# Gate and up sums as seven block products instead of eight, over two blocks of 512 rows, with streamed weights

## The chip, the cores and the metric

The kernel runs on one core of one Trainium2 chip. The metric is the device time of one execution in microseconds (us), median of the runs. All matrix work goes through TensorE; VectorE (DVE in the profile), ScalarE (ACT) and GpSimd (POOL) do the elementwise work, SyncE (SP) issues the DMAs. Each engine has one queue of instructions and works through it in order; a wait on a semaphore holds all that stands behind it in that queue.

## The reference

An array x of 2048 rows by 512 columns passes through five stages, each a residual update of x with a LayerNorm in front:

```
x = x + 0.5 * L0_ffn(layernorm(x))    # a 6-bit quantised 512x512 linear layer with bias
x = x + L0_attn(layernorm(x))         # causal convolution along the 512 columns, as a Toeplitz product
x = x + 0.5 * L0_ffn(layernorm(x))
x = x + 0.5 * L1_ffn(layernorm(x))    # the gated layer below
x = x + L1_attn(layernorm(x))         # convolution again, another filter
x = x + 0.5 * L1_ffn(layernorm(x))

def _L1_ffn_ref(x, W_gate, W_up, W_down):      # W_gate, W_up: 1376 x 512, W_down: 512 x 1376
    up = xt @ W_up.T
    gate = jax.nn.silu(xt @ W_gate.T)
    y = gate * up @ W_down.T
```

So there are six stages. The gated layer is run twice with the same weights; its hidden width 1376 is 10 blocks of 128 and one of 96. All arithmetic is float32.

## The kernel before

**Precision.** TensorE works in fp32r, a rounded float32. Each operand is therefore held as two parts, hi (the rounded value) and lo (the value minus hi), and each product is three matmuls: hi by hi, hi by lo, lo by hi. ScalarE makes hi by a copy, VectorE or GpSimd makes lo by a subtraction.

**Tiles and stages.** x stays in SBUF as 16 tiles of 128 rows (`x_rows`). Stages 0 to 2 (quantised, convolution, quantised) and 4 (convolution) are light: per tile 12 matmuls (`products`, L909 to L911), and 4 transposes of the normalised tile four items ahead (`transpose_step`, L312). Stages 3 and 5 are the gated layer.

**The way of a tile.** VectorE takes the statistics (`stats_step`, L271; `aggregate_step`, L281), GpSimd makes 1/sqrt(variance) and the shift by four tiny operations (`rstd_step`, L288 to L295), ScalarE normalises (`norm_step`, L305), TensorE transposes into a PSUM bank (L312), ScalarE rounds to `xt_hi` (L322), VectorE subtracts to `xt_lo` (L327), and after the products VectorE adds the sum to x (`update_step`, L335, L337). In the quantised stages GpSimd also adds a bias to each x tile (`bias_step`, L442) ahead of the update. Statistics run 7, GpSimd 6, the normalisation 5 (NORM_AHEAD) and the transposes 4 items ahead.

**Weights.** The gate, up and down weights are loaded once, in 32 chunks of 520 columns (`load_chunk`, L372), split while stages 1 and 2 run (ScalarE `chunk_hi_step` L534; lo on GpSimd L448 for the first 16 chunks, on VectorE L838 for the rest), and stay in SBUF, hi and lo, for both gated stages.

**Gated stages.** Four blocks of 512 rows each (BLK = 4 tiles), 11 steps f per block. In a step TensorE makes the gate and the up sum of hidden block f (`paired_sums`: stage 3 L997 to L1004, stage 5 L1008 to L1015; the first step of a stage `hidden_sums`, L980 to L982): 4 blocks of 128 input columns x 3 x 2 = 24 matmuls of 512 columns. Then it makes the down sums of step f-1 (`down`, L1038 to L1040): 4 row tiles x 3 = 12 matmuls, into the four `acc` banks, which add up over all 11 steps. Gate and up sums use four `front` banks, two a step in turn. Beside it ScalarE applies silu to the gate (L620), VectorE multiplies by up (L864), ScalarE rounds (L630), VectorE subtracts (L869). At a block's end 16 transposes prepare the next rows, then comes the last down.

**Code.** Stage 0 is straight code; stages 1 to 5 are loops over groups of four tiles or blocks (Fori), with the first block of each gated stage and the last of stage 5 apart.

## Time and profile before

| | |
|---|---|
| Time, median of 3 runs | 968.42 us (968.04 to 968.46) |
| Profiled execution | 968.6 us, span of its instructions 966.8 us |
| Busy: PE, DVE, ACT, POOL | 941.0, 361.5, 258.5, 189.6 us |
| Matmuls | 4376 |
| Mean granted TensorE clock | 0.996 |
| DMA moved | 21.70 MB, mean 22 GB/s |

How to read it: a share is busy time over the span. The duration that the profile gives for a matmul includes its way through the array, about 0.39 us for 512 columns, and the next one starts long before that; the cost of a matmul in a stream is the distance from its start to the next start. A granted clock of 1.0 means 2.4 GHz. Lines (L997) are lines of the kernel printed above.

### The profile page before, as it was taken

To read this page: it belongs to the slowest core of one execution; us is meant where nothing else is said; L and a number is where in the kernel's file an instruction comes from. 1 tells how busy PE (TensorE), PEld (TensorE's weight loads), DVE (VectorE), ACT (ScalarE), POOL (GpSimd) and SP (SyncE) were. 2 spreads that over 40 slices of the span, in tenths; PEclk is the share of its full clock that TensorE was granted. 3 is DMA by queue.
4 is the path that set the end of the run, shared out by engine and by line. 5 is a ranking of instruction groups with operands and counts; after the bars stand their busy time and mean duration, and the time that the engine had idled before them with its cause. 6 is when DMAs were issued, how large, how long until landed. Compare 5 with 4: busy or idle time off the path is not lost.

```text
span 966.8 us, 12613 instructions
## 1 busy us (share of the span) xinstructions
PE 941.0 (97%) x4376; PEld 771.8 (80%) x4376; DVE 361.5 (37%) x671; ACT 258.5 (27%) x415; POOL 189.6 (20%) x491
## 2 busy tenths in 40 slices
PE   3898999999999999999999999999999999999998
PEld 2675988888888878887888899888888788888886
DVE  6787869722132213221322286221321132223112
ACT  3432765422121212211221244121211122122111
POOL 5974899601000000100010033000000001000000
PEclk9999999999999999999999999999999999999999
DMA  8100333100000000000000000000100010001001
GB/s 311 67 1 0 89 96 89 58 1 1 0 1 1 1 1 0 0 0 0 0 0 0 0 0 1 1 1 1 44 0 1 1 43 0 0 0 44 1 1 43
DMA packets 10799, 21.70 MB, mean 22 GB/s; under 512 B 1040, under 2 KB 1296, under 8 KB 10768
## 3 DMA queue, kind: packets, MB, share of 16 engines
q1 hardware_dynamic: 10768, 21.28, 6.7%
q8 instruction: 20, 0.33, 0.1%
q14 instruction: 11, 0.09, 0.0%
HBM read 17.08 MB, written 4.19 MB: 22 GB/s over the span
## 4 chain that ended last, share of the span: by engine, by line
PE 86%; POOL 2%; DVE 1%; issue 1%; DMA 1%; ACT 1%; POOLq 0%; ACTq 0%; SPq 0%; DVEq 0%
PE acc L1038 8%; PE acc L1040 8%; PE acc L1039 8%; PE front L997 4%; PE front L1008 4%; PE front L1004 4%; PE front L1015 4%; PE front L998 4%; PE front L1009 4%; PE front L1000 4%; PE front L1013 4%; PE front L1010 4%; PE front L999 4%; PE front L1014 4%; PE front L1001 4%; PE front L312 3%
## 5 line engine op out<-in xcount | busy, mean ns | idle before, releaser
L864 DVE TENSOR_TENSOR gated<-front,gated 128x512 f32<-128x512 f32 (+1 forms) x88 | 60.8, 691 | 492.3 <-ACT gated L620 262.1
L620 ACT ACTIVATE gated<-front 128x512 f32<-128x512 f32 (+1 forms) x88 | 52.7, 599 | 493.5 <-PE front L1010 246.7
L288 POOL TENSOR_TENSOR minus_mean<-mean_var,constant_columns 128x1 f32<-128x1 f32 x98 | 25.3, 258 | 606.1 <-DVE mean_var L281 606.1
L1038 PE MATMUL acc<-ffn_w_hi,hidden_hi 128*128 128x512 f32 (+1 forms) x352 | 137.9, 392 | 0.0
L1040 PE MATMUL acc<-ffn_w_hi,hidden_lo 128*128 128x512 f32 (+1 forms) x352 | 137.0, 389 | 0.0
L1039 PE MATMUL acc<-ffn_w_lo,hidden_hi 128*128 128x512 f32 (+1 forms) x352 | 137.0, 389 | 0.0
L869 DVE TENSOR_TENSOR hidden_lo<-gated,hidden_hi 128x512 fp32r<-128x512 f32 (+1 forms) x88 | 60.9, 692 | 52.5 <-ACT hidden_hi L630 52.5
L305 ACT ACTIVATE normalised<-x_rows,minus_mean_rstd,rstd 128x512 f32 (+1 forms) x97 | 78.3, 808 | 4.4 <-POOL minus_mean_rstd L295 4.1
L322 ACT ACTIVATE xt_hi<-front 128x512 fp32r<-128x512 f32 x96 | 54.7, 595 | 89.5 <-PE front L312 89.4
L1040 PEld LDWEIGHTS acc<-ffn_w_hi,hidden_lo 128*128 128x128 f32 (+1 forms) x352 | 66.1, 188 | 14.1
L1039 PEld LDWEIGHTS acc<-ffn_w_lo,hidden_hi 128*128 128x128 f32 (+1 forms) x352 | 66.1, 188 | 14.0
L630 ACT ACTIVATE hidden_hi<-gated 128x512 fp32r<-128x512 f32 (+1 forms) x88 | 55.7, 633 | 80.7 <-DVE gated L864 80.7
L1038 PEld LDWEIGHTS acc<-ffn_w_hi,hidden_hi 128*128 128x128 f32 (+1 forms) x352 | 66.1, 188 | 13.9
L312 PE MATMUL front<-identity,normalised 128*128 128x128 f32 x384 | 57.1, 282 | 16.9 <-ACT normalised L305 16.8
L327 DVE TENSOR_TENSOR xt_lo<-front,xt_hi 128x512 fp32r<-128x512 f32 x96 | 63.9, 684 | 15.5 <-ACT xt_hi L322 14.4
L997 PE MATMUL front<-xt_hi,ffn_w_hi 128*128 128x512 f32 (+1 forms) x172 | 68.3, 397 | 0.0
L1008 PE MATMUL front<-xt_hi,ffn_w_hi 128*128 128x512 f32 (+1 forms) x172 | 68.3, 397 | 0.0
L1004 PE MATMUL front<-xt_hi,ffn_w_lo 128*128 128x512 f32 (+1 forms) x172 | 68.0, 396 | 0.0
L1015 PE MATMUL front<-xt_hi,ffn_w_lo 128*128 128x512 f32 (+1 forms) x172 | 68.0, 396 | 0.0
L998 PE MATMUL front<-xt_hi,ffn_w_hi 128*128 128x512 f32 (+1 forms) x172 | 67.4, 392 | 0.0
L1009 PE MATMUL front<-xt_lo,ffn_w_hi 128*128 128x512 f32 (+1 forms) x172 | 67.4, 392 | 0.0
L271 DVE BATCH_NORM_STATS2 bn_stats<-x_rows 128x6 f32 (+1 forms) x99 | 66.6, 673 | 1.8 <-DMA x_rows<-x_in 1.7
(148 smaller groups left out, 1654.9 us busy)
## 6 DMA issues: line engine op xcount, KB each, us to landing
gated<-wffn SPq DMA_DIRECT2D x32, 260.0 KB, 2.6
x_rows<-x_in SPq DMA_DIRECT2D x3, 1024.0 KB, 12.8
out<-x_rows SPq DMA_DIRECT2D x3, 1024.0 KB, 4.3
x_rows<-x_in SPq DMA_DIRECT2D x2, 512.0 KB, 6.3
q_raw<-qweight SPq DMA_DIRECT2D x4, 256.0 KB, 8.4
out<-x_rows SPq DMA_DIRECT2D x4, 256.0 KB, 2.1
omega_terms<-omega_in SPq DMA_DIRECT2D x1, 768.0 KB, 10.1
small_tables<-table_in SPq DMA_DIRECT2D x1, 517.0 KB, 10.7
```

What stands on the lines that cost most here:

```text
L271: nc.vector.bn_stats(bnst[:, slot, :], x_tile(t, ahead)).then_inc(stats_raw, 1)
L305: nc.scalar.activation(LN[:, slot, :], x_tile(t, ahead), ACT.Identity, bias=nmr[:, slot, :], scale=rstd[:, slot, :]).then_inc(norm_done, 1)
L312: last = nc.tensor.transpose(front[slot][:, j * P:(j + 1) * P], LN[:, slot, j * P:(j + 1) * P], ident[:])
L997: T.matmul(pair[0], hi[0], xh, start=first, stop=False)
L998: T.matmul(pair[1], hi[1], xh, start=first, stop=False)
L1004: up = T.matmul(pair[1], lo[1], xh, start=False, stop=final)
L1008: T.matmul(pair[0], hi[0], xh, start=first, stop=False)
L1009: T.matmul(pair[0], hi[0], xl, start=False, stop=False)
L1015: up = T.matmul(pair[1], lo[1], xh, start=False, stop=final)
L1038: T.matmul(acc[r][:], hh, Wh[:m, cols], start=(f == 0), stop=False)
L1039: T.matmul(acc[r][:], hh, Wl[:m, cols], start=False, stop=False)
L1040: last = T.matmul(acc[r][:], hl, Wh[:m, cols], start=False, stop=(f == FT - 1))
```

## The change

**Two blocks at a time.** A unit is now 8 tiles of 1024 rows: the tiles with an even place in the unit are one block of 512 rows (first half), the odd ones another (second half). There are 4 units: rows 0 to 1023 and 1024 to 2047, for each of the two gated stages. The gate and up sums of both row blocks are a 2 x 2 block product (gate and up by the two halves of the 512 input columns, by the two row blocks). Winograd's form of it takes 7 block products instead of 8, with 4 sums of weight blocks (S1 to S4) and 4 sums of row blocks (T1 to T3, T4N). Each product is 2 x 3 = 6 matmuls of 512 columns, so a step f has 42 matmuls where two blocks had 48. The products alternate between two PSUM banks (front 0 and 1). VectorE puts the four results together with seven adds, each of which reads a bank once.

**Weights are streamed.** SBUF no longer holds all of them. Each step loads 512 KB of gate and up weights (two slots) and each down pass 256 KB (three slots), in every unit again. Per step GpSimd makes four sums of 256 columns (`weight_sums`) and two subtractions of 1024 and 512 columns, ScalarE three roundings of 768, 1024 and 512, VectorE one subtraction of 768. The chunk splitting of stages 1 and 2 is gone.

**Down.** The first half's hidden blocks are rounded and summed as before, one step behind. The second half's hidden blocks (g1 x u1, made on GpSimd) are kept in float32 for all 11 steps (`second_hidden`, 22 KB a partition) and are rounded and summed in 11 passes after the steps, in the same four acc banks.

**Rows.** 8 tiles of a unit are prepared in 4 pairs (`pair_copies`, `pair_sums`, `pair_lows`, `sums_hi_step`, `sums_lo_step`): for unit 0 among the last items of stage 2, for the others between the down passes of the unit before. The layer-1 convolution (stage 4) is embedded in units 1 and 2: one item's products per step in steps 2 to 9, its transposes in steps 1 to 8. LayerNorm of coming items stands in the steps as the table `LN_OF_STEP` says. All code is straight, with no loops.

```diff
+UNITS = 4
+UTILES = 8
+STEPS = UNITS * FT
+PASSES = 2 * FT
+WD_RING = 3
...
+    after = {8: (0, 1), 10: (2, 3), 11: (4, 5), 12: (6, 7)}
+    for t in range(TILES):
+        light("quant", 0, t)
+        for p in after.get(t, ()):
+            prep(p)
...
+EMBEDDED = {0: 0, 1: UTILES, 2: UTILES, 3: 0}
+LN_OF_STEP = {u: {f: [] for f in range(FT)} for u in range(UNITS)}
+for _u in range(UNITS - 1):
+    for _e in range(EMBEDDED[_u]):
+        LN_OF_STEP[_u][_e].append(UNIT_ITEMS[_u] + _e)
+    for _s in range(BLK):
+        _f = 7 + _s if EMBEDDED[_u] else 3 + _s
+        for _i in range(2):
+            LN_OF_STEP[_u][_f].append(UNIT_ITEMS[_u] + EMBEDDED[_u] + 2 * _s + _i)
+PAIR_BEFORE_PASS = {-1: 0, 1: 1, 3: 2, 5: 3}
...
         @block.gpsimd
+            for n in range(PRE):
+                if ITEMS[n].kind == "quant":
+                    bias_step(n)
+                if n + RSTD_AHEAD < PRE:
+                    rstd_step(pool, n + RSTD_AHEAD)
...
+                if n + 3 < PRE and second_of_pair(n + 3):
+                    sums_lo_step(pool, ITEMS[n + 3].number // 2)
+                if n == PRE - 7:
+                    weight_sums(pool, 0)
+                if n == PRE - 4:
+                    weight_sum_lo(pool, 0)
+                    down_weight_lo(pool, 0)
...
+            def second_hidden(k):
+                f, u = k % FT, k // FT
+                pool.wait_ge(silu_done, 2 * k + 2)
+                pool.wait_ge(front_read, READS * k + C22)
+                if u:
+                    pool.wait_ge(hid_ready, PASSES * (u - 1) + FT + f + 1)
+                TT(H1[:, f, :], g1, u1, ALU.mult).then_inc(h1_made, 1)
+            for u in range(UNITS):
+                for f in range(FT):
+                    k, q = FT * u + f, PASSES * u + f
+                    if f:
+                        second_hidden(k - 1)
+                    if k + 1 < STEPS:
+                        weight_sums(pool, k + 1)
+                    down_weight_lo(pool, q + 1)
+                    if k + 1 < STEPS:
+                        weight_sum_lo(pool, k + 1)
+                    for n in LN_OF_STEP[u][f]:
+                        rstd_step(pool, n)
...
         @block.scalar
+            for u in range(UNITS):
+                for f in range(FT):
+                    k, q = FT * u + f, PASSES * u + f
+                    if f:
+                        silu(k - 1, g1, C12)
+                    snapshot(k)
+                    silu(k, g0, C11)
+                    if k + 1 < STEPS:
+                        weight_raw_hi(act, k + 1)
+                        weight_sum_hi(act, k + 1)
+                    down_weight_hi(act, q + 1)
+                    if 1 <= f <= EMBEDDED[u]:
+                        xt_hi_step(act, embedded_item(u, f - 1))
+                    for n in LN_OF_STEP[u][f]:
+                        norm_step(act, n)
+                    act.wait_ge(first_made, k + 1)
+                    hidden_hi(q, g0)
+                silu(FT * u + FT - 1, g1, C12)
+                if u + 1 < UNITS:
+                    pair_copies(act, BLK * (u + 1))
+                second_hidden_hi(u, 0)
+                for j in range(FT):
+                    q = PASSES * u + FT + j
+                    if u + 1 < UNITS and j in (0, 2, 4, 6):
+                        sums_hi_step(act, BLK * (u + 1) + j // 2)
+                    if q + 1 < UNITS * PASSES:
+                        down_weight_hi(act, q + 1)
+                    if u + 1 < UNITS and j in (1, 3, 5):
+                        pair_copies(act, BLK * (u + 1) + (j + 1) // 2)
+                    if j + 1 < FT:
+                        second_hidden_hi(u, j + 1)
...
         @block.vector
+                    first_gate(k)
+                    middle_sums(k)
+                    if k + 1 < STEPS:
+                        weight_raw_lo(dve, k + 1)
+                    if f == 0 and u:
+                        for r in range(BLK):
+                            ffn_update(u - 1, 1, r)
...
+                    first_hidden(k)
+                    second_gate(k)
+                    hidden_lo(q, g0)
+                q1 = PASSES * u + FT
+                hidden_lo(q1, H1[:, 0, :])
+                if u + 1 < UNITS:
+                    pair_sums(dve, BLK * (u + 1))
+                for r in range(BLK):
+                    ffn_update(u, 0, r)
+                if u + 1 < UNITS:
+                    pair_lows(dve, BLK * (u + 1))
+                for j in range(1, FT):
+                    hidden_lo(q1 + j, H1[:, j, :])
+                    if u + 1 < UNITS and j in (2, 4, 6):
+                        pair_sums(dve, BLK * (u + 1) + j // 2)
+                        pair_lows(dve, BLK * (u + 1) + j // 2)
...
         @block.tensor
+            for u in range(UNITS):
+                for f in range(FT):
...
+                    pe.wait_ge(w_raw_ready, k + 1)
...
+                    product(k, M1, A11, B11)
...
+                    product(k, M2, A12, B21)
...
+                    pe.wait_ge(w_sum_ready, k + 1)
+                    pe.wait_ge(snap_done, k + 1)
+                    product(k, M6, S2, T2)
+                    pe.wait_ge(front_read, READS * k + C11)
+                    product(k, M5, S1, T1)
+                    pe.wait_ge(front_read, READS * k + U2)
+                    product(k, M7, S3, T3)
+                    if 2 <= f < 2 + EMBEDDED[u]:
+                        embedded_products(embedded_item(u, f - 2))
...
+                    elif f:
+                        down(q - 1, ALL)
+                    if 1 <= f <= EMBEDDED[u]:
+                        embedded_transposes(embedded_item(u, f - 1))
+                    pe.wait_ge(front_read, READS * k + T_SUM)
+                    product(k, M4, A22, T4N)
+                    pe.wait_ge(front_read, READS * k + C22)
+                    product(k, M3, S4, B22)
...
+                for j in range(-1, FT - 1):
+                    if u + 1 < UNITS and j in PAIR_BEFORE_PASS:
+                        pair_transposes(BLK * (u + 1) + PAIR_BEFORE_PASS[j])
+                    down(PASSES * u + FT + j, ALL)
```

In the names: M1 to M7 are the products; C11, C12 the gate sums g0 and g1 of the two halves, C21, C22 the up sums; U2, U3 and T_SUM sums between. `snapshot` is ScalarE's copy of M1 out of its bank; M6 writes that bank next. The first half's hidden block g0 x up is made on VectorE (`first_hidden`), rounded by `hidden_hi` and subtracted by `hidden_lo`.

## Rows read from the trace of the kernel before

**Rows 1.** busy us, share of the span, and instructions by engine, from the page

```profile
PE 941.0 (97%) x4376; PEld 771.8 (80%) x4376; DVE 361.5 (37%) x671; ACT 258.5 (27%) x415; POOL 189.6 (20%) x491
```

**Rows 2.** table by stage: us, each engine's busy (instructions), PEclk, DMA share, GB/s

```profile
25.00:50.00 25.00, 23.11 (x105) 18.28 (x106) 18.94 (x35) 11.50 (x19) 23.01 (x63) 0.93 0.14 52
200.00:225.00 25.00, 25.00 (x111) 20.50 (x110) 6.25 (x13) 5.11 (x8) 2.14 (x8) 1.00 0.00 1
```

**Rows 3.** TensorE's longest wait: total us, times, longest

```profile
PE front L312 <- ACT normalised L305: 16.8, 6, 10.9
```

**Rows 4.** timeline of TensorE, stage 3: start us, duration, engine, line, operation

```profile
300.77 0.39 PE L997 MATMUL front<-xt_hi,ffn_w_hi 128*128 128x512 f32 x1
...
306.30 0.39 PE L1038 MATMUL acc<-ffn_w_hi,hidden_hi 128*128 128x512 f32 x1
...
309.03 0.39 PE L997 MATMUL front<-xt_hi,ffn_w_hi 128*128 128x512 f32 x1
```

**Rows 5.** chain that ended last, light stages: start us, us, what

```profile
108.39 0.55 POOL rstd L292
...
110.98 0.55 POOL rstd L292
...
140.06 0.44 PE front L312 x4
143.27 0.44 PE front L312 x4
...
560.91 0.46 PE front L312 x4
563.25 0.46 PE front L312 x4
```

**Rows 6.** groups by line and shape, VectorE and ScalarE: busy, mean ns, idle before

```profile
L869 DVE TENSOR_TENSOR hidden_lo<-gated,hidden_hi 128x512 fp32r<-128x512 f32 x80 | 55.4, 692 | 46.3 <-ACT hidden_hi L630 46.3
...
L793 DVE TENSOR_TENSOR toeplitz_f<-toeplitz_f,small_tables 128x128 f32<-128x128 f32 x2 | 0.6, 291 | 0.1
...
L305 ACT ACTIVATE normalised<-x_rows,minus_mean_rstd,rstd 128x512 f32 x72 | 58.2, 809 | 0.3
...
L630 ACT ACTIVATE hidden_hi<-gated 128x512 fp32r<-128x512 f32 x80 | 50.6, 633 | 73.5 <-DVE gated L864 73.5
...
L558 ACT ACTIVATE silu_of_a_constant<-constant_columns 128x1 f32<-128x1 f32 x1 | 0.2, 202 | 0.0
```

**Rows 7.** the same view for GpSimd, 128 columns

```profile
L483 POOL TENSOR_TENSOR inv_den_r<-den_r,den_tmp 128x128 f32<-128x128 f32 x4 | 1.8, 458 | 0.0
```

**Rows 8.** timeline of VectorE and GpSimd, stage 2, where two operations meet

```profile
141.18 1.29 POOL L442 TENSOR_TENSOR x_rows<-x_rows,half_bias 128x512 f32 x1
...
141.60 1.43 DVE L838 TENSOR_TENSOR ffn_w_lo<-gated,ffn_w_hi 128x520 f32 x1
...
142.43 0.65 POOL L288 TENSOR_TENSOR minus_mean<-mean_var,constant_columns 128x1 f32<-128x1 f32 x1
```

**Rows 9.** timeline of GpSimd, stage 2: one rstd_step and one bias_step

```profile
178.56 0.19 POOL L288 TENSOR_TENSOR minus_mean<-mean_var,constant_columns 128x1 f32<-128x1 f32 x1
...
179.80 1.29 POOL L442 TENSOR_TENSOR x_rows<-x_rows,half_bias 128x512 f32 x1
181.06 0.18 POOL L288 TENSOR_TENSOR minus_mean<-mean_var,constant_columns 128x1 f32<-128x1 f32 x1
```

**Rows 10.** DMA issues: queue, count, KB each, median us from issue to landing

```profile
gated<-wffn SPq DMA_DIRECT2D x32, 260.0 KB, 2.6
...
out<-x_rows SPq DMA_DIRECT2D x3, 1024.0 KB, 4.3
```

**Rows 11.** timeline of TensorE, stage 0, after a gap

```profile
27.10 0.66 PE L312 MATMUL front<-identity,normalised 128*128 128x128 f32 x4 [1.14 <-ACT normalised L305]
...
27.83 0.63 PE L910 MATMUL acc<-dequant_lo,xt_hi 128*128 128x512 f32 x1
...
30.81 0.59 PE L911 MATMUL acc<-dequant_hi,xt_lo 128*128 128x512 f32 x1
```

1095 lines of the change are left out of this document (606 added, 489 removed).

## The prediction

> **What bounds the kernel now.** I read the page's busy shares first: TensorE is busy 941.0 of 966.8 us, every other engine under 40% [rows 1]. That number can hide gaps, since matmul ends are modelled, so I read the table by stage next [rows 2]: in a feed-forward stretch (200 to 225 us) TensorE is busy all 25 us, VectorE 6.25, ScalarE 5.11, GpSimd 2.14. The list of TensorE's waits confirms it: 16.8 us in all behind the first normalised tiles and nothing in the feed-forward blocks [rows 3]. So the pitch of the matmuls is the price of the work. In the timeline [rows 4] 24 gate and up matmuls take 306.30 - 300.77 = 5.53 us, 0.2304 each, and 12 down matmuls 309.03 - 306.30 = 2.73 us, 0.2275 each. Eight blocks of 11 x 36 such matmuls are the 740 us that matter. The reader should see two things: removed matmuls are worth their full pitch, and the other engines have much free time but have so far handed over only once per 8.3 us.
>
> **What is removed.** Before: 8 blocks x 11 x 24 = 2112 gate and up matmuls. After: 4 units x 11 steps x 7 products x 6 = 1848. 264 fewer, x 0.2304 = 60.8 us. The pitch of the new products is not in the trace; its nearest rows are the old gate and up matmuls (0.2304, the same as now: no further gain) and the down matmuls (0.2275: 1848 x 0.0029 = 5.4 us more). I take the middle, 2.7. The downs, the 96 items' transposes and the light matmuls keep their number. The layer-1 convolution moves into steps 1 to 9 of units 1 and 2 at its own TensorE price: 2.34 us an item [rows 5], bound by TensorE then and later, so zero; nothing has to hide it.
>
> The weight split leaves the light stages. In the first convolution GpSimd's chunk set the pace, 110.98 - 108.39 = 2.59 us an item, where the second needs 563.25 - 560.91 = 2.34 [rows 5]: 16 x 0.25 = 4, of which I take 3 (0 to 4). Gains together: 60.8 + 2.7 + 3 = 66.5 us (61 to 70).
>
> **What is added, per step.** One step is 42 x 0.2304 + 12 x 0.2275 = 12.4 us of TensorE (14.7 with an embedded item). Sizes come from two rows each [rows 6], [rows 7]: VectorE 0.29 at 128 columns and 0.69 at 512, so 0.43 at 256 and 0.96 at 768; ScalarE 0.20 at one and 0.63 at 512, so 0.42 at 256 and 1.06 at 1024; GpSimd 0.46 at 128 and 1.29 at 512, so 0.74 at 256 and 2.40 at 1024. Per step VectorE has nine operations of 0.69 and one of 0.96, 7.2 us; ScalarE 4 x 0.63, 0.63, 0.85 and 1.06, 5.1; GpSimd 1.29 + 4 x 0.74 + 1.29 + 2.40 = 7.9. All fit under 12.4. The products themselves alternate between two banks: a product lasts 1.38 us and its last add 0.69 + 0.2, so each bank is free in time; M7's two adds and M5's are covered by the down sums that stand behind M7. So a bare step costs nothing by throughput; what costs is the order on each queue.
>
> The long loop runs ScalarE, GpSimd, ScalarE: second_hidden 1.29, weight_sums 3.1 with its waits, then weight_sum_hi and down_weight_hi 1.9 (GpSimd's down_weight_lo waits for both), 1.29, weight_sum_lo 2.40; VectorE's first_hidden 0.7 and add C12 0.7; silu of g1 0.7, which second_hidden of the next step waits for. That is 12.1 us, against 12.4.
>
> **The shared resource.** The timeline shows a VectorE subtraction of two SBUF operands take 1.43 us instead of 0.69: it begins 0.42 us into a GpSimd operation and ends 0.56 after it; GpSimd's next tiny operation in turn takes 0.65 instead of 0.19, up to VectorE's end [rows 8]. Per step three VectorE operations are of that kind (weight_raw_lo, first_hidden, hidden_lo). weight_raw_lo falls beside down_weight_lo and pushes weight_sum_lo by about 0.8: the loop becomes 12.9, 0.5 over TensorE. In 15 plain steps 0 to 8 us; I take 4.5, since the loop must first use up some slack. The Trainium skill, "SBUF — State Buffer", section "Who interferes with whom", calls this an exclusive lock held for the whole instruction. By it the wait behind a 1024-column weight_sum_lo or sums_lo could be the whole of it, which no row shows; that is the lock rival below.
>
> **LayerNorm in the steps.** rstd_step stands last on GpSimd's step, norm_step on ScalarE stands ahead of hidden_hi, and hidden_hi ahead of silu(g1) and of the next snapshot, for which M6 waits. A rstd_step is 179.80 - 178.56 = 1.24 us [rows 9], a norm 0.81 [rows 6]. With two items the loop is 12.9 + 2.5 + 0.8 + 0.6 - 1.4 (the adds no longer on it) = 15.4, less about 0.3 because operations queued back to back overlap: 15.1. Unit 0 has four such steps over 12.4: 4 x 2.7 - 2 of first slack = 8.5 us (5 to 11). Units 1 and 2: step 0, where four updates wait for the down sums and sit ahead of C21, 2; step 1, 1; step 7 with three items against 14.7, 1.5; steps 8 and 9, 0.5: 5 each, 10 together (6 to 16).
>
> **The second half of a unit.** 11 down passes of 2.73 us. Ahead of the first, on ScalarE, stand pair_copies (four operations, 1.5 to 1.8 us), which wait for the transposes, then the hidden's rounding; on VectorE hidden_lo, then pair_sums (1.7), then the updates that free the acc banks. Counted from the transposes' end: 1.5 + 0.7 + 0.7 + 1.7 + 0.7 = 5.3 us to the first freed bank, under 2.6 us of down sums: 2.7 late. For each later pair the loop copies 1.5, rounding 0.7, hidden_lo 0.6, pair_sums 1.7, sums_hi 1.0, and three half-us roundings is 7.0 us, against 2 x 2.73 + 0.9 = 6.4, and hidden_lo of the odd pass waits for sums_lo (2.40) to end, 1 to 2 us. Together 8.6 us for the change from unit 0. In units 1 and 2, step 10 still has two norms ahead of hidden_hi, so the last first-half hidden and the copies come some 4 us later: 12 each. Sum 33 (18 to 42). Unit 3 has no pairs: 0. A down weight's load (256 KB, 2.6 us to landing [rows 10]), ScalarE 0.6 and GpSimd 1.3 make 4.6 us after the pass that frees its slot, against two passes, 5.5: hidden, though only just. The 512 KB load of a step is put between 2.6 and 4.3 (260 and 1024 KB, [rows 10]), and has most of a step; it stands behind a down load whose wait ends earlier.
>
> **The end of the light part.** Eight preparation items stand among the last 15. An item of the quantised stage leaves GpSimd 0.7 us (2.50 of 3.21, [rows 9], [rows 5]). From item 38 on GpSimd has 12 x 1.24 + 7 x 1.29 + 4 x 2.40 (sums_lo) + 3.1 (first weight_sums) = 36.6 us before bias_step of item 50 has gone through, and xt_lo of items 54 and 55 stands behind that item's update on VectorE; TensorE wants them after 28 us and cannot run far ahead, because each preparation item waits for its pair. I take 12 us (4 to 14). The opening steps add 1.5.
>
> **The clock.** After a gap of 1.14 us TensorE ran eight matmuls 0.43 us apart [rows 11], the lower of its two levels (1.2 against 2.4 GHz); the granted clock of that stretch is 0.93 [rows 2]. Where it idles behind a loop of other engines the slower matmuls are absorbed; I add 3.5 us (0 to 25).
>
> **Sum.** 968.6 (the profiled execution; span 966.8, 0.2 over the median 968.42) - 66.5 + 4.5 + 8.5 + 10 + 33 + 12 + 1.5 + 3.5 = 975.1. Forecast: 975, slightly slower.
>
> **Rivals.** (1) The hand-offs hide. Should ScalarE and GpSimd pipeline better than my single file, the costs take their lower ends: 0 + 5 + 6 + 18 + 4 + 1 + 0 = 34, so 936, or 932 with the better pitch. For it: the free shares of [rows 2]; I followed queues in strict order with full latencies. Against: each chain is written out in the queues. (2) The lock decides, the slower side. From the point where second_hidden ends later than 5 us into a step, first_hidden meets weight_sum_lo from its beginning: 2.4 us before C12 instead of 0.5, in all 40 steps some 1 us more, 40 us: 1015. Against: VectorE may come first and push GpSimd instead, which costs 0.7. (3) The clock: 25 gaps over 1 us, each with 8 slower matmuls x 0.2 = 1.6, cost 40 rather than 3.5, half of it absorbed: 995. (4) The change does not do what it says, as weights come late: 44 loads, 1 us late each, 44 us less slack: 1000. Against: landing near 3.4 us in a 12.4 us step.
>
> **Chances.** Forecast 0.45, rival 1 0.33, rival 2 0.09, rival 3 0.09, rival 4 0.04. About 0.2% (2 us) is what a measurement of this kernel tells from no change. All of rival 1 and 0.05 of the forecast's share are faster, 0.05 lies within: faster 0.38, same 0.05, slower 0.57. The forecast's own range is 958 to 992. With both signs held, the range is 937 to 1005: it leaves out rival 1's lower edge and rival 2's.
>
> **What would show it.** Right: idle time of TensorE at M6 behind the snapshot in steps with LayerNorm, at the first second-half pass behind the updates, at the last light items behind xt_lo; steps near 12.9 and 15 us, the change of units 9 to 12 us over 27 + 2.7. Wrong: those waits absent and steps at 12.4 (rival 1); first_hidden with a mean over 1.5 us (rival 2); granted clock under 0.95 through the units (rival 3); waits on DMA at the weight roundings (rival 4). The saving itself is wrong if the products' pitch is off 0.23.

## The result, and the profile after

The changed kernel takes 996.6 us (median of 4 runs, 995.2 to 997.8) against 968.4: a ratio of 1.029 (1.027 to 1.031). The forecast was 975 us, slightly slower. The sign holds, and so does the range of 937 to 1005 us that takes in the rivals. The forecast's own range, 958 to 992, is missed, and so is the size: +28 us where +6.5 was forecast. I compare the two profiled executions, 996.6 and 968.6 us, whose spans differ by the same 28.0 us. One execution of one kernel below fell into a slower state of the chip (1361.6 us at a granted clock of 0.61) and is left out.

The head of the page, which answers [rows 1]:

```profile
span 994.8 us, 11946 instructions
PE 903.6 (91%) x4088; PEld 731.2 (74%) x4088; DVE 642.2 (65%) x1021; ACT 410.9 (41%) x650; POOL 634.4 (64%) x835
```

TensorE has less to do and is no longer always busy; VectorE and GpSimd went from 37% and 20% of the span to 65% and 64%. No engine but TensorE is near full, and the 91% still hides gaps. The same table by stage as [rows 2], with one more stretch:

```profile
25.00:50.00 25.00, 23.51 (x109) 19.15 (x110) 18.36 (x34) 12.46 (x20) 23.46 (x62) 0.93 0.21 83
200.00:225.00 25.00, 23.14 (x96) 18.35 (x95) 13.87 (x18) 8.11 (x12) 15.33 (x16) 0.95 0.07 22
175.00:200.00 25.00, 15.76 (x68) 12.55 (x69) 13.09 (x29) 12.34 (x19) 20.14 (x35) 0.85 0.00 0
```

From 175 to 200 us TensorE has work for 15.76 of 25 us, and its granted clock is 0.85: that is the end of the light part. Its waits, which answer [rows 3] (total, times, longest):

```profile
PE front L440 <- ACT normalised L433: 19.0, 9, 4.4
PE acc L1245 <- DVE hidden_lo L1118: 16.2, 13, 4.1
PE front L1291 <- DVE snapshots L1084: 12.1, 9, 3.1
PE front L1291 <- ACT snapshots L839: 10.1, 8, 2.3
PE front L440 <- DMA identity<-table_in: 9.3, 1, 9.3
PE acc L1245 <- POOL down_lo L569: 9.1, 9, 1.1
```

Before, nothing in the feed-forward blocks appeared in this view. Now the down passes wait for `hidden_lo` and `down_lo`, the products for the snapshot and the gate and up sums, the transposes for the norm. None waits on a weight load directly, though ScalarE's rounding of down weights does, 40.9 us in 23 times, 20 of them in the down passes behind the steps, and `down_lo` comes behind it.

The pitch, the counterpart of [rows 4]: four products of six matmuls in step 3 of unit 1 (start, duration; two such rows per product).

```profile
442.66 0.39 PE L1291 MATMUL front<-row_operands_hi,weight_operands_hi 128*128 128x512 f32 x1
...
444.02 0.39 PE L1291 MATMUL front<-row_operands_hi,weight_operands_hi 128*128 128x512 f32 x1
...
448.10 0.39 PE L1291 MATMUL front<-row_operands_hi,weight_operands_hi 128*128 128x512 f32 x1
```

Six matmuls take 1.36 us, 0.2267 each, a little better than the middle I took (about 0.229). A bare step therefore costs 54 x 0.2267 = 12.24 us, one with an embedded item 14.63.

What the steps really take is read from the first product's row in steps 4, 5, 6 and 7 of unit 0:

```profile
254.50 0.47 PE L1291 MATMUL front<-row_operands_hi,weight_operands_hi 128*128 128x512 f32 x1 [0.17 <-DVE snapshots L1084]
271.90 0.47 PE L1291 MATMUL front<-row_operands_hi,weight_operands_hi 128*128 128x512 f32 x1 [0.70 <-DVE snapshots L1084]
285.54 0.47 PE L1291 MATMUL front<-row_operands_hi,weight_operands_hi 128*128 128x512 f32 x1
302.95 0.47 PE L1291 MATMUL front<-row_operands_hi,weight_operands_hi 128*128 128x512 f32 x1 [0.71 <-DVE snapshots L1084]
```

17.4, 13.6, 17.4 us instead of 12.24. With every step read like this, the 28.0 us lie as follows. The first feed-forward product starts at 205.07 instead of 185.33: 19.7 us later. From there to the last matmul it is 786.2 us instead of 777.9: 8.3 us more, made of some 69 us saved (60.8 by matmuls not run, 8 by pitch) and some 80 us of steps and passes over their TensorE time, which agrees to 3 us. TensorE's time is counted at 0.2267 us a matmul, 2.39 an embedded item and 0.1 a transpose:

| Stretch | over TensorE's time | forecast |
|---|---|---|
| End of the light part | 24 (5 ahead when the second quantised stage began, 19.7 late at the end) | 12 (4 to 14) |
| Unit 0, steps 3 to 7 (LayerNorm in them) | 13.7 | 8.5 (5 to 11) |
| Units 1 and 2, steps 0 to 9 | 15 | 10 (6 to 16) |
| Three unit changes, with the step ahead of each | 40 | 33 (18 to 42) |
| Plain steps and the rest, unit 3 and the first step among them | 11 | 6: 4.5 (0 to 8) and 1.5 for the opening steps |

### The profile page after: what moved, and what is told of

Read it like the earlier page. It is cut to its first block, busy times and chain, and to the rows that moved or that the text cites. A ratio compares the mean times of both kernels' runs of the same rounds, so it can differ in the third digit from the quotient of the medians.

```text
span 994.8 us, 11946 instructions
## 1 busy us (share of the span) xinstructions
PE 903.6 (91%) x4088; PEld 731.2 (74%) x4088; DVE 642.2 (65%) x1021; ACT 410.9 (41%) x650; POOL 634.4 (64%) x835
## 4 chain that ended last, share of the span: by engine, by line
PE 55%; POOL 19%; DVE 12%; ACT 6%; issue 6%; DMA 3%; SPq 0%; POOLq 0%; DVEq 0%; ACTq 0%
PE front L1291 10%; PE front L1293 10%; PE front L1292 10%; PE acc L1245 5%; PE acc L1247 5%; PE acc L1246 4%; POOL down_lo L569 3%; POOL row_operands_lo L516 3%; POOL w_and_weight_operands_lo L559 3%; PE front L440 2%; PE acc L1185 2%; POOL rstd L422 2%; PE acc L1184 2%; PE acc L1183 2%; DVE w_and_weight_operands_lo L554 2%
## 5 line engine op out<-in xcount | busy, mean ns | idle before, releaser
L1291 PE MATMUL front<-row_operands_hi,weight_operands_hi 128*128 128x512 f32 x616 | 247.4, 402 | 23.1 <-DVE snapshots L1084 12.1
L1293 PE MATMUL front<-row_operands_hi,w_and_weight_operands_lo 128*128 128x512 f32 x616 | 243.5, 395 | 0.0
L1292 PE MATMUL front<-row_operands_lo,weight_operands_hi 128*128 128x512 f32 x616 | 243.3, 395 | 0.0
L569 POOL TENSOR_TENSOR down_lo<-raw_down,down_hi 128x512 fp32r<-128x512 f32 x88 | 131.8, 1499 | 141.6 <-ACT down_hi L564 133.0
L1245 PE MATMUL acc<-down_hi,hidden_hi 128*128 128x512 f32 x352 | 143.0, 406 | 27.1 <-DVE hidden_lo L1118 16.2
L1291 PEld LDWEIGHTS front<-row_operands_hi,weight_operands_hi 128*128 128x128 f32 x616 | 117.6, 191 | 58.6 <-issue 28.0
L1247 PE MATMUL acc<-down_hi,hidden_lo 128*128 128x512 f32 x352 | 138.8, 394 | 0.0
L1246 PE MATMUL acc<-down_lo,hidden_hi 128*128 128x512 f32 x352 | 138.8, 394 | 0.0
L1292 PEld LDWEIGHTS front<-row_operands_lo,weight_operands_hi 128*128 128x128 f32 x616 | 117.6, 191 | 23.3
L559 POOL TENSOR_TENSOR w_and_weight_operands_lo<-raw_weights,weight_operands_hi 128x1024 fp32r<-128x1024 f32 x44 | 117.6, 2672 | 0.0
L1247 PEld LDWEIGHTS acc<-down_hi,hidden_lo 128*128 128x128 f32 x352 | 66.9, 190 | 14.6
L440 PEld LDWEIGHTS front<-identity,normalised 128*128 128x128 f32 x384 | 47.0, 146 | 38.2 <-issue 14.6
## 6 DMA issues: line engine op xcount, KB each, us to landing
x_rows<-x_in SPq DMA_DIRECT2D x3, 1024.0 KB, 13.6
```

The costliest lines, as they stand in the source:

```text
L440: last = nc.tensor.transpose(o[:, j * P:(j + 1) * P], LN[:, n % LN_SLOTS, j * P:(j + 1) * P], ident[:])
L559: nc.gpsimd.tensor_tensor(flat(Wl, k, 1 + S1, 2 + S4), flat(Wr, k, 1 + S1, 2 + S4), flat(Wh, k, S1, S4 + 1).bitcast(F32), ALU.subtract).th ...
L569: nc.gpsimd.tensor_tensor(WDl[:, q % WD_RING, :], WDr[:, q % WD_RING, :], WDh[:, q % WD_RING, :].bitcast(F32), ALU.subtract).then_inc(wd_r ...
L1245: T.matmul(acc[r][:], hh, wh, start=(f == 0), stop=False)
L1246: T.matmul(acc[r][:], hh, wl, start=False, stop=False)
L1247: last = T.matmul(acc[r][:], hl, wh, start=False, stop=(f == FT - 1))
```

## The experiments

Each kernel below is the changed one with the edit shown; times are medians of 4 runs (3 in one case), beside 996.6 for the changed kernel. The kernel before, run again beside each of them, took 967.9 to 968.2. They are told nearly in the order in which they were run. "The steps" are the distances between first products, as above; step 10, the last, ends where the first down pass behind it starts, and "the passes" run from there to the next unit.

**Order in the light part.** VectorE, ScalarE and GpSimd:

```
-    pair_sums(dve, ...); pair_lows(dve, ...)
     aggregate_step(dve, n + STATS_AHEAD)
+    pair_sums(dve, ...); pair_lows(dve, ...)
...
+    sums_hi_step(act, ...)
     norm_step(act, n + NORM_AHEAD)
-    sums_hi_step(act, ...)
...
-    if n + 3 < PRE and second_of_pair(n + 3):
+    if n + 2 < PRE and second_of_pair(n + 2):
         sums_lo_step(pool, ...)
```

> Light part only: VectorE's aggregate stands ahead of the pair's sums instead of behind them, ScalarE's rounding of the pair sums ahead of the next norm, and GpSimd's sums_lo one item later, behind the next bias addition. No operation is added or removed. If the stall at the end of the light part (about 23 us in the changed kernel) comes from a ring of in-order queues (aggregate behind pair sums, rstd behind the aggregate, norm behind rstd, bias behind sums_lo), the first feed-forward product comes 8 to 15 us earlier than 205 us and the time is 982 to 989 us. If GpSimd's sheer work there is the bound, nothing moves: 995 to 998 us.

Measured 982.5 (980.3 to 986.1), 14.1 less; the first product starts at 194.22 instead of 205.07. The ring can be read in the changed kernel on one pair. GpSimd, after its bias addition, idles for VectorE's `aggregate`; then, much later, the 2.35 us `sums_lo` stands ahead of the next bias addition:

```profile
164.58 1.28 POOL L689 TENSOR_TENSOR x_rows<-x_rows,half_bias 128x512 f32<-128x512 f32 x1
168.26 0.19 POOL L418 TENSOR_TENSOR minus_mean<-mean_var,constant_columns 128x1 f32<-128x1 f32 x1 [2.40 <-DVE mean_var L413]
...
171.79 2.35 POOL L516 TENSOR_TENSOR row_operands_lo<-pair_sums,row_operands_hi 128x1024 fp32r<-128x1024 f32 x1 [2.30 <-ACT row_operands_hi L512]
174.10 1.26 POOL L689 TENSOR_TENSOR x_rows<-x_rows,half_bias 128x512 f32<-128x512 f32 x1
```

VectorE's aggregate stood behind the six operations of a pair (from 165.62 on) and began at 168.01; its next update but one waited 3.94 us for the bias addition. The waits between 145 and 205 us, of the changed kernel and of this one:

```profile
POOL minus_mean L418 <- DVE mean_var L413: 10.6, 6, 4.1
DVE x_rows L462 <- POOL x_rows L689: 20.6, 6, 7.4
PE front L440 <- ACT normalised L433: 13.3, 5, 4.4
```

```profile
POOL minus_mean L418 <- DVE mean_var L413: 4.1, 3, 3.0
DVE x_rows L462 <- POOL x_rows L689: 7.0, 4, 3.5
PE front L440 <- ACT normalised L433: 7.7, 4, 2.3
```

With not one operation fewer, 11 of the 24 us go. The stretch that my term added up can be read too: from GpSimd's bias addition of item 38 to that of item 50, in the changed kernel and in this one.

```profile
147.88 1.29 POOL L689 TENSOR_TENSOR x_rows<-x_rows,half_bias 128x512 f32<-128x512 f32 x1
...
195.19 1.28 POOL L689 TENSOR_TENSOR x_rows<-x_rows,half_bias 128x512 f32<-128x512 f32 x1
```

```profile
148.32 1.29 POOL L689 TENSOR_TENSOR x_rows<-x_rows,half_bias 128x512 f32<-128x512 f32 x1
...
183.38 1.27 POOL L689 TENSOR_TENSOR x_rows<-x_rows,half_bias 128x512 f32<-128x512 f32 x1
```

To the end of the second row that is 48.6 us in the changed kernel, of which GpSimd idles 15, and 36.3 us here, close to the 36.6 of my sum. So GpSimd's work was not what made the stretch long, since GpSimd itself stood idle. What remains (13 us) is close to the 12 I took, but I did not take it apart; nor the 3 us that the units gain in this kernel, where nothing was moved.

**The norm behind the rounding.**

```
-    for n in LN_OF_STEP[u][f]: norm_step(act, n)
     act.wait_ge(first_made, k + 1)
     hidden_hi(q, g0)
+    for n in LN_OF_STEP[u][f]: norm_step(act, n)
```

> In every step the LayerNorm of the items prepared there is put on ScalarE behind the rounding of the first hidden rows instead of ahead of it. Theory: in steps 3 to 6 of unit 0 and step 10 of units 1 and 2 the norms, which wait for GpSimd's rstd, delay hidden_hi, silu of g1 and the next snapshot; they cost 13.7 + 2 x 5.2 us there. Then this gives 12 to 20 us back: 976 to 985 us. Rival: those steps are long because GpSimd's own queue is (rstd behind a weight_sum_lo of 2.67 us, lengthened by VectorE's shared access): 0 to 4 us, 992 to 997 us.

Measured 1001.0 (1000.0 to 1001.8), 4.4 more. My theory fell: steps 3 to 7 of unit 0 are unchanged to 0.06 us. Silu of g1 and the snapshot stand behind the norm wherever in the step it is put, and the norm waits for its rstd. In units 1 and 2, step 10 fell to 15.4 but the passes after it grew from 41.7 to 45.5 us and more: the wait only moved.

**The updates first, at the unit change.**

```
-    pair_copies(act, BLK * (u + 1))
     second_hidden_hi(u, 0)
+    pair_copies(act, BLK * (u + 1))
...
-    pair_sums(dve, BLK * (u + 1))
     for r in range(BLK): ffn_update(u, 0, r)
+    pair_sums(dve, BLK * (u + 1))
```

> At each unit change the first second-half hidden rows are rounded ahead of the pair's four copies on ScalarE, and the four row updates stand ahead of the pair's sums on VectorE. Theory: the order of the two queues makes the first passes late, 2 to 4 us at each of three changes: 984 to 991 us. Rival: the passes are late because VectorE's hidden_lo waits for GpSimd's long sums_lo and ScalarE's copies for each other, whatever the order: within 2 us of the changed kernel, 994 to 998 us. A loss is possible if the pair's sums, now later, hold the next transposes.

Measured 1001.9 (998.2 to 1003.7), 5.3 more: the loss that I had called possible, but the rows suggest another reason (only a part of it, as the smaller edits on top of the three moves show). ScalarE in this kernel:

```profile
356.96 0.39 ACT L482 ACTIVATE row_operands_hi<-front 128x256 fp32r<-128x256 f32 x1
361.32 1.06 ACT L512 ACTIVATE row_operands_hi<-pair_sums 128x1024 fp32r<-128x1024 f32 x1 [3.97 <-DVE pair_sums L500]
362.29 0.61 ACT L564 ACTIVATE down_hi<-raw_down 128x512 fp32r<-128x512 f32 x1
362.80 0.61 ACT L848 ACTIVATE hidden_hi<-second_hidden 128x512 fp32r<-128x512 f32 x1
```

The rounding of the pair's sums waits 3.97 us for VectorE, and the roundings of the down weight and of the next hidden rows, whose inputs are there, stand behind it. In the changed kernel the same wait is 2.21 us. That gave the theory for "The roundings ahead of the pair", below.

**All three.**

> The three reorderings (light part, LayerNorm in the steps, unit change) together. If queue order is the cause of all three stalls and they are independent, the gains add: 25 to 45 us, 952 to 972 us, which would be level with or below the kernel before (968.4). If throughput of GpSimd or the shared access decides, 985 to 997 us.

Measured 988.8 (987.6 to 991.2): 7.8 less than the changed kernel, where the sum of the three alone is -14.1 + 4.4 + 5.3 = -4.4. Nearly additive: the moves hardly help or hinder each other.

**rstd ahead of the long remainder.** On GpSimd, in steps without an embedded item's products:

```
+    for n in LN_OF_STEP[u][f] if early else (): rstd_step(pool, n)
     weight_sum_lo(pool, k + 1)
-    for n in LN_OF_STEP[u][f]: rstd_step(pool, n)
+    for n in () if early else LN_OF_STEP[u][f]: rstd_step(pool, n)
```

> The changed kernel with one move on GpSimd: in the steps without an embedded convolution item (all of unit 0, step 10 of units 1 and 2) the rstd of the prepared items stands ahead of weight_sum_lo (2.4 to 3.1 us) instead of behind it. ScalarE's order is as in the changed kernel. Theory: it is not the place of the norm on ScalarE that counts (moving it gave nothing) but when rstd is there, since silu of g1 and the snapshot stand behind the norm wherever it is put. Then the four long steps of unit 0 (13.0, 17.4, 13.6, 17.4, 13.5 us against 12.24) and step 10 of units 1 and 2 (18.3 against 14.63) come down to within 1.5 us of their floor each: 980 to 988 us. Rival: weight_sum_lo, 2.5 us later, now delays M6 by as much: 994 to 1000 us.

Measured 974.5 (973.8 to 976.1), 22.1 less. In the changed kernel GpSimd runs as follows, then ScalarE:

```profile
251.28 3.12 POOL L559 TENSOR_TENSOR w_and_weight_operands_lo<-raw_weights,weight_operands_hi 128x1024 fp32r<-128x1024 f32 x1
254.36 0.19 POOL L418 TENSOR_TENSOR minus_mean<-mean_var,constant_columns 128x1 f32<-128x1 f32 x1
...
257.02 0.19 POOL L425 TENSOR_TENSOR minus_mean_rstd<-minus_mean,rstd 128x1 f32<-128x1 f32 x1
259.24 1.28 POOL L755 TENSOR_TENSOR second_hidden<-gate_up 128x512 f32<-128x512 f32 x1 [2.02 <-ACT gate_up L843]
```

```profile
256.13 0.82 ACT L433 ACTIVATE normalised<-x_rows,minus_mean_rstd,rstd 128x512 f32<-128x512 f32 x1 [6.17 <-POOL minus_mean_rstd L425]
257.31 0.81 ACT L433 ACTIVATE normalised<-x_rows,minus_mean_rstd,rstd 128x512 f32<-128x512 f32 x1 [0.36 <-POOL minus_mean_rstd L425]
258.03 0.61 ACT L848 ACTIVATE hidden_hi<-gate_up 128x512 fp32r<-128x512 f32 x1
258.55 0.61 ACT L843 ACTIVATE gate_up<-gate_up 128x512 f32<-128x512 f32 x1
259.06 0.57 ACT L839 ACTIVATE snapshots<-front 128x512 f32<-128x512 f32 x1
```

ScalarE idles 6.17 us for the rstd; the snapshot comes last, and TensorE's third product starts at 259.78, 2.28 us late. Behind that gap, from 260.88 on, it ran 8 matmuls at half speed, 0.43 us apart (its granted clock is 0.66 from 260 to 265 us). Here, GpSimd makes the same rstd ahead of the long operation, and the steps of unit 0 read:

```profile
252.60 0.47 PE L1294 MATMUL front<-row_operands_hi,weight_operands_hi 128*128 128x512 f32 x1
266.06 0.39 PE L1294 MATMUL front<-row_operands_hi,weight_operands_hi 128*128 128x512 f32 x1
278.70 0.39 PE L1294 MATMUL front<-row_operands_hi,weight_operands_hi 128*128 128x512 f32 x1
291.31 0.39 PE L1294 MATMUL front<-row_operands_hi,weight_operands_hi 128*128 128x512 f32 x1
```

13.5, 12.6, 12.6 us. All of unit 0 gives back 10.8 us, and units 1 and 2 4.0 and 4.6. Most of that lies in their first two steps: in unit 1 15.1 and 15.1 us become 13.1 and 13.3, and the next grows from 14.8 to 15.7. The expectation speaks of step 10 only, but the edit also moves the rstd of the embedded items that steps 0 and 1 prepare.

**The roundings ahead of the pair.** On ScalarE, in the second half:

```
-    sums_hi_step(act, ...)
     down_weight_hi(act, q + 1)
-    pair_copies(act, ...)
     second_hidden_hi(u, j + 1)
+    sums_hi_step(act, ...)
+    pair_copies(act, ...)
```

> The changed kernel with one move on ScalarE in the second half of a unit: the down weight's rounding and the next hidden rows' rounding stand ahead of the pair's rounding of sums (which waits for VectorE's pair sums) and of the next pair's copies (which wait for the transposes), instead of behind them. Theory: the passes of a unit change are late because these roundings wait behind sums_hi, which is why putting the updates ahead of the pair's sums lost 2 to 4 us a change. Then each change (41.6 us for 32.6 of TensorE) falls by 3 to 6 us and the time is 980 to 989 us. Rival: GpSimd's long sums_lo and the shared access set the passes whatever ScalarE does: 993 to 998 us.

Measured 977.8 (975.8 to 980.4), 18.8 less: the passes of the three changes fall from 41.6, 41.7, 42.1 to 35.6, 36.3, 36.9 us, of 32.6 that TensorE needs. So it was ScalarE's order more than GpSimd's `sums_lo` that made them late.

**The long remainders in four pieces.**

```
-    nc.gpsimd.tensor_tensor(flat(Wl, k, 1 + S1, 2 + S4), ..., ALU.subtract)
+    for i in range(4):
+        last = nc.gpsimd.tensor_tensor(flat(Wl, k, 1 + S1 + i, 2 + S1 + i), ..., ALU.subtract)
```

> The changed kernel with each 1024-column rounding remainder on GpSimd (weight_sum_lo and sums_lo) as four of 256 columns, 4 x 0.74 = 2.96 us instead of 2.4. If VectorE's two-operand subtractions and first_hidden wait for the end of a whole GpSimd instruction, their longest durations fall from 2.6 us to some 1.4, their means towards 0.9, and the long operation, lengthened to 3.1 when they come first, gains nothing: in time a gain of 2 to 8 us, 989 to 995. If the delay is one of sharing in small pieces, or none of these is on the path, the 0.55 us more per step decides: 997 to 1003 us.

Measured 994.8 (993.0 to 998.7), 1.8 less, hardly beyond the spread. In the trace the longest second-half `hidden_lo` falls from 2.77 to 1.39 us, the longest `first_hidden` from 2.17 to 1.29. So VectorE does wait for the end of a whole GpSimd instruction, as one of the long waits behind `sums_lo` in the changed kernel shows too:

```profile
362.77 2.36 POOL L516 TENSOR_TENSOR row_operands_lo<-pair_sums,row_operands_hi 128x1024 fp32r<-128x1024 f32 x1
```

```profile
363.05 2.63 DVE L1118 TENSOR_TENSOR hidden_lo<-second_hidden,hidden_hi 128x512 fp32r<-128x512 f32 x1
```

It begins 0.28 us into GpSimd's operation and ends 0.55 us after it. By the Trainium skill's rule of a lock held for the whole instruction ("SBUF — State Buffer", "Who interferes with whom") that is what should happen, and the trace agrees. But shorter pieces buy almost nothing in time. Two effects work against each other: the mean of VectorE's `weight_raw_lo` falls from 1.70 to 1.31 us, and GpSimd's four pieces take 3.37 us together where the whole took 2.67, 0.70 more per step, where 0.55 was expected. How much each is worth was not measured apart.

**An eighth product.** The six matmuls of M3 run twice into the same bank, in each of the 44 steps.

> The changed kernel with an eighth product in each of its 44 steps: the six matmuls of M3 are run twice into the same bank, so nothing else changes. It prices a removed product. At full pitch 44 x 1.36 = 59.8 us. Theory: TensorE is the bound in most steps, only the long steps of unit 0 (and step 10 and the first steps after a change) absorb theirs: plus 45 to 57 us, 1042 to 1054 us. Rival: the loop through ScalarE and GpSimd sets the steps and most of the saving was never to be had: plus 5 to 30 us, 1002 to 1027 us.

Measured 1025.8 (1023.6 to 1026.9): 29.2 more, of 59.8 at full pitch. It lies in the rival's range, at its upper end, and far from my theory's 45 to 57. Steps that took 12.24 to 12.65 take exactly 13.60; the long ones swallow it (unit 0's steps 4 to 7 fall from 61.9 to 60.7 in all), and its granted clock rises from 0.976 to 0.987. Half of what the change saves is lost at once to waits that a busier TensorE does not have.

**The three moves together** (light part, rstd, roundings).

> The three moves that gave time alone, together: light part (14.1 us alone), rstd ahead of weight_sum_lo (22.1), ScalarE's roundings ahead of the pair's (18.8). If they mend three stalls in separate places they add: 996.6 - 55.0 = 941.6 us (938 to 948), under the kernel before (968). If they share a cause (the lower clock after a gap, or one move only shifting a wait to where another helps), the sum is less: 950 to 965 us.

Measured 947.3 (946.4 to 948.2), ratio to the kernel before 0.979 (0.977 to 0.980): faster than both. It has 49.3 of the 55.0 us of the sum, and the same 11946 instructions as the changed kernel.

**On top of these, three smaller edits**: the updates first at the unit change; the long remainders in four pieces; and the light part's pairs placed later:

```
-    after = {8: (0, 1), 10: (2, 3), 11: (4, 5), 12: (6, 7)}
+    after = {8: (0, 1), 10: (2, 3), 12: (4, 5), 14: (6, 7)}
```

> The three moves and the unit-change order that lost 5 us when put alone (the updates ahead of the pair's sums, the second half's first rounding ahead of the pair's copies). Theory: it lost only because sums_hi, which waits for the pair's sums, stood ahead of the next roundings; with that gone it frees the banks earlier and gives 1 to 5 us over the three moves alone. Rival: it loses by itself, since the pair's remainders free the transposes' banks later: plus 2 to 5 us.

> The three moves, with weight_sum_lo and sums_lo in four pieces each. With the queue order mended, the remaining waits at the first passes after a pair are VectorE's hidden_lo behind a whole sums_lo: minus 2 to 6 us against the three moves alone. If GpSimd's loop is what is left, the 0.55 us more per step costs plus 1 to 5 us.

> The three moves, and the light part's last pairs one and two items later (after tiles 12 and 14 instead of 11 and 12). If the pairs' density still makes the end of the light part late, minus 2 to 6 us against the three moves alone; if the last pair, now closer to the first feed-forward product, is on its path, plus 1 to 5 us.

Measured 951.8, 951.8 and 948.6, against 947.3. The updates first lose 4.4 even with the roundings moved, so my reason for their loss when put alone was not all of it: in units 1 and 2 the passes still grow by 1.9 and 1.3 us. The pieces lose 4.5: unit 1 grows by 4.1 us (its step 8 takes 18.7 instead of 16.2), units 0 and 2 by 2.0 and 1.4, and unit 3 gains 4.5. With the pairs placed later the first product starts 2.1 us earlier (190.36 instead of 192.44), but unit 0 grows by 2.8, most of it in its first step: the gain only moves.

**The eighth product in the mended kernel.**

> The kernel with the three moves (947.3 us) with the six matmuls of M3 run twice in each of the 44 steps. If queue order was what absorbed half of a product's price in the changed kernel (29.2 of 59.8 us), it is charged nearly in full here: plus 44 to 56 us, 991 to 1003 us. If the other engines' sheer work absorbed it, plus 28 to 38 us, 975 to 985 us.

Measured 982.3 (980.0 to 984.6), 35.0 more than the three moves. So mending the orders raised what a product costs only from 29.2 to 35.0 of 59.8. That lies in the range of the second alternative: these three orders were not what absorbed most of the price. The other engines' own work is what is left as its cause, which no run shows by itself. Read the other way, the new form with the matmuls of eight products costs 982 us, 14 more than the kernel before, and leaving one out brings it to 947. Two of its steps in unit 0:

```profile
244.47 0.39 PE L1294 MATMUL front<-row_operands_hi,weight_operands_hi 128*128 128x512 f32 x1
258.07 0.39 PE L1294 MATMUL front<-row_operands_hi,weight_operands_hi 128*128 128x512 f32 x1
271.67 0.39 PE L1294 MATMUL front<-row_operands_hi,weight_operands_hi 128*128 128x512 f32 x1
```

13.60 us each, TensorE's own time, with a granted clock of 0.997 in the mean. With eight products the steps of unit 0 hide all other work, LayerNorm too; with seven, TensorE's 12.24 us are just under the 12.6 that the same steps take.

**No LayerNorm in step 10 of units 1 and 2** (eight pair items by 2, 3, 3 in steps 7 to 9).

> The kernel with the three moves, with the eight pair items of units 1 and 2 prepared in steps 7, 8, 9 (2, 3, 3) instead of 7 to 10 (2 each), so that step 10 holds no LayerNorm. If the last step's 17.55 us (14.63 by TensorE) come from the norms ahead of hidden_hi there, it falls to 14.7 in both units, and steps 8 and 9 take back 1 to 3 us: minus 2 to 5 us, 942 to 945. If the last hidden rows' own chain (first_hidden, rounding, remainder, then the pass) sets it, as step 10 of unit 0 with 14.75 would say against, nothing: 946 to 950.

Measured 949.6 (948.8 to 950.4), 2.3 more. Step 10 only falls to 17.3 and 16.4, and step 9 rises from 14.5 to 15.7: step 10 stays long with no norm in it. In step 9 ScalarE waits 5.74 us for the first rstd, and the rounding of its hidden rows stands behind the three norms. That this lateness is what reaches into step 10 is my reading; no run isolates it.

**VectorE's raw remainder nearly taken away.** In `weight_raw_lo` the slices end at 96 of 768 columns, and `product` takes the high part twice for the raw operands; first in the changed kernel, then with the three moves:

```
-    nc.vector.tensor_tensor(flat(Wl, k, 1, 4), flat(Wr, k, 1, 4), ...)
+    nc.vector.tensor_tensor(flat(Wl, k, 1, 4)[:, 0:96], flat(Wr, k, 1, 4)[:, 0:96], ...)
```

> The changed kernel, no order touched, with VectorE's weight_raw_lo on 96 of 768 columns, and the raw weights' low part left out of the products (the high part is multiplied twice, so TensorE's work is the same). It takes away the operation that meets GpSimd's in every step (1.70 us mean, 0.96 alone). By the forecast its push is worth some 0.5 us a step in the plain steps and a little in the long ones: minus 2 to 6 us, 991 to 995. If the shared access makes the long steps of unit 0 long, they lose 1 to 3 us each, minus 8 to 15 us: 982 to 989. If the loop has slack for it everywhere, nothing: 995 to 998.

> The kernel with the three moves (947.3 us) with weight_raw_lo on 96 of 768 columns and the raw weights' low part left out of the products (the high part twice), which took 16 us off the changed kernel. If the operation and what it meets on the shared access are what keeps the mended steps over TensorE's floor (12.6 against 12.24, 13.3 to 17.5 in the first, ninth and last steps), minus 8 to 16 us, 931 to 939. If the three moves have already taken that part, minus 0 to 4 us, 943 to 948.

Measured 980.1 (978.0 to 981.0), 16.5 less; and 935.2 (932.9 to 936.5), 12.1 less than 947.3. The groups of the changed kernel and of the first of these two:

```profile
L554 DVE TENSOR_TENSOR w_and_weight_operands_lo<-raw_weights,weight_operands_hi 128x768 fp32r<-128x768 f32 x44 | 74.7, 1697 | 0.0
L559 POOL TENSOR_TENSOR w_and_weight_operands_lo<-raw_weights,weight_operands_hi 128x1024 fp32r<-128x1024 f32 x44 | 117.6, 2672 | 0.0
```

```profile
L554 DVE TENSOR_TENSOR w_and_weight_operands_lo<-raw_weights,weight_operands_hi 128x96 fp32r<-128x96 f32 x44 | 35.7, 811 | 0.0
L559 POOL TENSOR_TENSOR w_and_weight_operands_lo<-raw_weights,weight_operands_hi 128x1024 fp32r<-128x1024 f32 x44 | 105.6, 2400 | 0.0
```

An operation of 96 columns takes 0.81 us in the mean, and up to 2.34, far more than the 0.29 of 128 columns of [rows 6]: most of it is waiting for GpSimd. GpSimd's `weight_sum_lo` drops to the 2.40 I had estimated. The plain steps fall to 12.24 us, most of unit 3's among them. So one operation of VectorE and its meetings with GpSimd are worth 12 to 17 us. How much of that is its own length on VectorE and how much the meeting, these runs do not part.

**The norm one step later.** Pair items only: their norm stands behind the next step's silu of g0, the last step's behind silu of g1.

```
     silu(k, g0, C11)
+    for n in LN_OF_STEP[u][f - 1] if f else ():
+        if not is_light(n): norm_step(act, n)
```

> The kernel with the three moves, and each pair item's norm on ScalarE in the next step, behind the snapshot and silu of g0, where its rstd has long been made; the last step's norms stand behind silu of g1 and ahead of the pair's copies. If norms waiting for a late rstd hold hidden_hi and silu of g1 in steps 9 and 10 of units 1 and 2 (17.55 against 14.63), these fall by 1 to 3 us each and unit 0's step 4 by 1: minus 4 to 9 us, 938 to 943. If the norms ahead of the first copies make the unit change later by as much, 946 to 950.

Measured 943.6 (942.4 to 944.7), ratio to before 0.975 (0.973 to 0.977), the best. Step 8 of units 1 and 2 falls from 16.2 to 14.6, and that is where the gain comes from. Step 10 falls from 17.55 to 13.54, but the passes behind grow from 35.2 and 36.3 to 40.2 and 40.4, so that the two together gain nothing in either unit. The last norms, 1.5 us, now stand ahead of the copies; what makes up the rest was not followed up.

## Why the prediction was right and wrong

The forecast came out 21.5 us low. Too small were the end of the light part (by 12), the unit changes (7), LayerNorm in unit 0, units 1 and 2 and the plain steps (5 each); against that the pitch gave 5 more and the earlier light stages 2 more (5 for 3), and the 3.5 for the clock was no term of its own. Added up this is 23.5, as near to 21.5 as the counting goes. That the total still lies in the wide range says little, since every term of cost but the clock's missed the same way. Two slips in the working are small: 4 x 2.7 - 2 is 8.8, not 8.5, and 2.6 + 0.6 + 1.3 is 4.5, not 4.6.

**The saving** was right: 60.8 us by count, and the pitch gave some 8 instead of 2.7. The middle between two rows was the cautious choice and cost 5.

**End of the light part: the term that was mis-sized most**, 24 for 12. The failing step is the sum "= 36.6 us before bias_step of item 50 has gone through": I added up GpSimd's operations as if it were never idle. The stretch took 48.6 us, 12 more, and GpSimd was idle for 15 of them; between 145 and 205 us it waited 10.6 us for VectorE's aggregate. I had not written the order of aggregate, rstd, norm and bias out for a pair; with another order the same operations took 36.3 us, and the whole kernel 14.1 less.

**LayerNorm in unit 0**, 13.7 for 8.5. The loop I wrote, with rstd behind `weight_sum_lo`, was right: a pair of steps takes 17.4 + 13.6 = 31.0, 15.5 each, against 15.1 forecast for the loop. Its size was off: steps 4 to 7 are 3.2 us over on average where I had 2.7, with the slow matmuls after the gap in every second one, and the slack of 2 us that I deducted was not there, since step 3 is already 0.7 over. Moving the rstd confirmed the loop.

**Units 1 and 2**, 15 for 10: inside the bounds. Most lies in steps 0, 1 and 8. The embedded items themselves (steps 3 to 7) cost nothing, as forecast: 14.63 to 14.66.

**The unit changes**, 40 for 33: right in kind (first pass behind updates and `hidden_lo`). I named pair copies and pair sums as the chain, and missed that `sums_hi`, which waits for VectorE, stands ahead of roundings whose inputs are there: moving these took 16.6 us off the passes of the three changes. "Hidden, though only just", of a down weight's load, was wrong at the edge: TensorE waits 9.1 us, nine times, for `down_lo`, in part behind a load.

**Plain steps**, 11 for 4.5, or for 6 with the opening steps' 1.5; in it are unit 3's first two steps, 2.0 and 1.7, and the very first, 2.3. A typical plain step alternates between 12.24 and 12.65: up to 0.4 over, as forecast (0.5). The shared access behind that term is real, and with it the operation is worth 12 to 17 us over the whole kernel, more than the 4.5 I gave it (which stood for its push only, not for its own time on VectorE).

**The clock**, 3.5 as a term of its own. In the units some 60 matmuls start about 0.43 us apart, the lower level, some 12 us over their pace in sum; before it was none. With the three moves it is some 20 (4 us). The runs of them that I read stand behind gaps. This is part of the sizes above and must not be added to them. The third rival's 995 is the measured time, but its cause isn't: some 12 us of slow matmuls, not 40, and the reorderings remove most of them together with the gaps. The near hit is luck.

**The first rival** (hand-offs hide, 936) was wrong for the kernel as written. The mended ones come near it, with 947.3 and 943.6. **The second** (lock, 1015) did not come: `first_hidden` has a mean of 0.86, under the 1.5 set as its mark. **The fourth** (late weights, 1000) put 1 us on each of 44 loads, and that did not come. GpSimd's `weight_sums` wait 13.2 us in 21 times for gate and up weights, but 10 of these stand in steps 3 to 7 of units 1 and 2, which run at TensorE's 14.63. Its sign, waits on DMA at the weight roundings, did appear in the passes behind the steps. In the change from unit 0, ScalarE:

```profile
390.01 0.63 ACT L564 ACTIVATE down_hi<-raw_down 128x512 fp32r<-128x512 f32 x1 [1.99 <-DMA raw_down<-wdown]
```

and the pass behind it, on TensorE:

```profile
392.09 0.47 PE L1245 MATMUL acc<-down_hi,hidden_hi 128*128 128x512 f32 x1 [1.00 <-POOL down_lo L569]
```

So loads take part in the lateness of the passes. They set little of it: with the roundings moved ahead of the pair ScalarE waits for these loads more often (48.7 us in 40 times), and TensorE for `down_lo` less (2.2 us in 3).

## What to carry to other kernels

When an engine that was the only busy one loses work, price each hand-off by writing the order of all queues out for one period, with the idle time of each engine in it, not by adding up the busiest helper's operations: here 49 of the 68.5 us saved hung on the order alone. Put what waits for another engine behind what waits for nothing, on each queue; and ask of every move what stands behind the wait at its new place, since two of five single moves only shifted it. And test a saving by adding it back: an eighth product cost 29 of 60 us, which says in one run that TensorE alone is no longer the bound.

## What the runs showed of the hardware

Two-operand subtractions in SBUF on VectorE and GpSimd stretch each other to the end of the other's instruction: up to 2.77 us for 0.69, 3.12 for 2.40, and 0.81 in the mean for 96 columns. Cutting GpSimd's operation in four halves the longest second-half `hidden_lo` (2.77 to 1.39 us) and leaves its mean nearly as it was (1.28 and 1.14 us), while the four pieces of `weight_sum_lo` take 0.70 us more than the whole. Of TensorE's clock: a gap of 2.28 us behind ScalarE's snapshot was followed by 8 matmuls at the 1.2 GHz level, and in the kernels with fewer gaps the mean granted clock is higher: 0.976 in the changed kernel, 0.993 with the three moves, 0.997 with an eighth product on top of them.
